# A transformer layer on one core: the first unit's keys, queries and maxima moved by 0/1 matrices instead of by DRAM, x and weights given turned, projections moved into the cycles

## What is computed

```python
x = _layernorm(x + attention(x))      # 32 query heads of width 16, 8 groups of keys and values, causal
x = _layernorm(x + ffn(x))

# attention: q = x Wq, k and v = x Wkv; scores = q k^T, upper triangle left out
# weights = softmax(scores / 4); out = (weights v) Wo + bo
# ffn:
h = einsum('bsd,nrd->nbsr', x, lora_A)
lora_out = einsum('nbsr,nor->bso', h, lora_B * 2 * lora_weights)
out = einsum('bsd,od->bso', x, W) + bias + lora_out
```

## Time and profile before

| | us |
|---|---|
| median of 3 runs (344.4 to 345.73) | 344.89 |
| the profiled execution | 345.44 |
| its span, first to last instruction | 343.7 |
| PE busy, share of the span | 327.0, 95% |
| DVE busy | 256.6, 75% |
| ACT busy | 219.9, 64% |
| POOL busy | 122.7, 36% |

### The profile page before, as it was taken

How to read it: one execution, slowest core, us unless ns; L and a number is a source line. 1 busy time by engine, 2 the same in 40 slices (tenths; PEclk the granted TensorE clock), 3 DMA queues, 4 the chain that set the end, 5 groups by cost and what they waited for, 6 DMA issues and landing times.

```text
span 343.7 us, 7378 instructions
## 1 busy us (share of the span) xinstructions
PE 327.0 (95%) x2584; PEld 180.8 (53%) x2585; DVE 256.6 (75%) x786; ACT 219.9 (64%) x414; POOL 122.7 (36%) x251
## 2 busy tenths in 40 slices
PE   7897989999999999999999999999999999999993
PEld 3674645555555454454454454544545545458882
DVE  2427788798889988978989889799888971037664
ACT  3672265676667768766847858588587686962331
POOL 2364233476455445511321114121141122321553
PEclk9999999999999999999999999999999999999999
DMA  7939948432450111010010010000000000000002
GB/s 217 267 121 194 340 115 97 109 97 83 136 141 14 36 50 47 2 49 0 3 47 32 3 48 3 1 32 3 1 2 1 16 18 3 2 10 23 0 31 93
DMA packets 21316, 21.38 MB, mean 62 GB/s; under 512 B 6112, under 2 KB 17312, under 8 KB 21280
## 3 DMA queue, kind: packets, MB, share of 16 engines
q1 hardware_dynamic: 21280, 20.92, 23.1%
HBM read 14.68 MB, written 6.03 MB: 60 GB/s over the span
## 4 chain that ended last, share of the span: by engine, by line
PE 81%; SPq 4%; DVE 4%; DMA 4%; ACT 3%; issue 3%; POOL 1%; POOLq 0%; DVEq 0%; ACTq 0%
PE PS L1195 20%; PE PS L1053 18%; PE PS L1031 18%; PE PS L1217 17%; SPq L468 2%; PE PS L1123 2%; PE PS L1115 2%; DMA TC<-in_L_attn_Wkv_dram 2%; ACT PB L772 1%; PE PS L1099 1%; DMA QS<-NMR 1%; PE PS L1101 1%; DMA QS<-scr_q 1%; PE PS L1040 1%; DVE scrap L829 1%
## 5 line engine op out<-in xcount | busy, mean ns | idle before, releaser
L772 ACT ACTIVATE PB<-PS 128x512 f32<-128x512 f32 x288 | 154.9, 600 | 55.9 <-PE PS L1217 54.5
L829 DVE CUSTOM_DVE_ANT_0 scrap<-PS,mask 128x128 bf16<-128x128 f32 (+3 forms) x256 | 111.6, 487 | 16.7 <-PE PS L1031 16.0
L1031 PE MATMUL PS<-KS,QS 96*128 96x512 bf16 (+3 forms) x384 | 107.2, 329 | 2.4 <-DMA QS<-scr_q 1.5
L1217 PE MATMUL PS<-QS,KS 99*128 99x512 bf16 x288 | 106.1, 381 | 0.8 <-ACT VX L673 0.3
L822 DVE TENSOR_REDUCE MX<-PS 128x1 f32<-128x512 f32 x128 | 82.1, 684 | 12.5 <-PE PS L1031 11.6
L648 POOL TENSOR_SCALAR_AFFINE_SELECT PB<-PB 128x256 f32<-128x256 f32 (+1 forms) x96 | 46.2, 483 | 105.5 <-ACT PB L772 102.5
L1195 PE MATMUL PS<-PB,VX 128*32 128x256 f32 (+1 forms) x1280 | 78.8, 364 | 0.6 <-ACT PB L772 0.3
L1031 PEld LDWEIGHTS PS<-KS,QS 96*128 96x128 bf16 x384 | 32.9, 98 | 47.9 <-issue 11.8
L1195 PEld LDWEIGHTS PS<-PB,VX 128*32 128x32 f32 x1280 | 33.5, 109 | 39.0 <-issue 16.1
L1053 PE MATMUL PS<-XT,WQ 128*128 128x512 f32 x144 | 41.5, 420 | 2.1 <-DVE WQ L966 1.5
L1217 PEld LDWEIGHTS PS<-QS,KS 99*128 99x128 bf16 x288 | 27.4, 98 | 30.3 <-ACT PB L772 7.1
(11 more groups left out here) (84 smaller groups left out, 270.2 us busy)
## 6 DMA issues: line engine op xcount, KB each, us to landing
scr_q<-parts SPq DMA_DIRECT2D x8, 384.0 KB, 2.9
QS<-scr_q SPq DMA_DIRECT2D x16, 192.0 KB, 3.5
X<-in_L_attn_x_dram SPq DMA_DIRECT2D x8, 256.0 KB, 5.7
QS<-scr_q SPq DMA_DIRECT2D x16, 128.0 KB, 3.3
out_dram<-TC SPq DMA_DIRECT2D x8, 256.0 KB, 2.0
QS<-scr_q SPq DMA_DIRECT2D x16, 64.0 KB, 3.1
...
```

The costliest lines, as they stand in the source:

```text
L772: nc.scalar.activation(PB[:, cyc % NP_BUF, k, :], PS[:, score_bank(e), :], ACT.Exp, scale=SCALE)\
L829: last = nc.vector.tensor_tensor_reduce(out=scrap[:, n % 2, (j - j0) * width:(j - j0 + 1) * width], in0=bank[:, j - j0, :], in1=mask[:, HT ...
L1031: last = nc.tensor.matmul(PS[:, CHUNK_BANK[n], k * width:(k + 1) * width], QS[0:ROWS, u % SLOTS, j, qb * P:(qb + 1) * P], KS[0:ROWS, g, k0 ...
L1217: nc.tensor.matmul(PS[:, score_bank(e), :], KS[0:NROW, u % G, kb * P:(kb + 1) * P], QS[0:NROW, u % SLOTS, heads[0]:heads[-1] + 1, s * HQ + ...
```

## The change

Five things change. (1) The host gives x turned as well as plain, Wq with its columns in the order of `parts`, Wkv as keys and values apart, lora_B and W turned, and the lora weights one to a partition. The `xT` and `bT` jobs and the transposes in `WE` go; ACT and DVE (first half) or POOL (second half) make the high and low part from x turned in SBUF, and plain x is loaded over it later, in cycles 8 to 16. (2) For unit 0, K and Q reach their rows by PE: POOL builds 0/1 selectors out of the identity, three matmuls of 96x512 place group 0's keys (`direct_keys`), twelve place the four heads (`direct_queries`), and 16 of 3x128 place the maxima (`direct_rows`), each copied by ACT or DVE from PSUM to `KS` or `QS`. The other units go through DRAM as before. (3) The last Q of the first half and V's transposes of the second move from the opening into cycles 2 and 6, the other fillers of `LATER` follow in cycles 5 to 17. (4) `WE` is one float32 matmul; DVE adds W, ACT copies the high part two cycles later and POOL subtracts the low part. (5) The idle matmuls behind `xT` and before cycle 0 go; the maxima of units 2 and 3 are turned one cycle later; Wo, LoRA and bias loads, and the splits of Wo and x, stand in other cycles.

The diff, cut to what the text speaks of:

```diff
-        return (FIRST[u] - (LEAD if u > 1 else 2)) if u else -1
+        return (FIRST[u] - (LEAD if u > 3 else 2)) if u else -1
...
-    PLAN_A = [(("xT", 0, c), 0) for c in range(NC)]
-    PLAN_A += [(("K", 0, 0), 0), (("Q", 0, 0), 0), (("V", 0, 0), 0), (("Q", 0, 1), 0), (("VT", 0, 0), 0)]
-    PLAN_A += [(("xT", 1, c), 0) for c in range(NC)]
-    PLAN_A += [(("Q", 0, 2), 5), (("K", 1, 0), 11), (("V", 1, 0), 13), (("Q", 0, 3), 15), (("VT", 1, 0), 16)]
+    PLAN_A = [(("K", 0, 0), 0), (("Q", 0, 0), 0), (("V", 0, 0), 0), (("Q", 0, 1), 3), (("VT", 0, 0), 4),
+              (("Q", 0, 2), 9), (("K", 1, 0), 11), (("V", 1, 0), 14)]
...
-    ROWS0_AFTER = 15
-    LATER = [("Q", 1, c) for c in range(NC)] + [("bT", 0, 0)] + [("WE", 0, c) for c in range(NC)]
+    LATER = [("Q", 0, 3), ("Q", 1, 0), ("VT", 1, 0), ("Q", 1, 1), ("WE", 0, 0), ("Q", 1, 2), ("WE", 0, 1),
+             ("Q", 1, 3), ("WE", 0, 2), ("WE", 0, 3)]
...
-    FILL = dict(zip((2, 5, 8, 11, 13, 14, 17, 20, 22), LATER))
+    FILL = dict(zip((2, 5, 6, 8, 10, 11, 13, 14, 16, 17), LATER))
...
-    LORA_AT, W_AT, SCALE_AT = (1, 2, 4, 5), (7, 10), 7
...
+    WO_AT, LORA_AT, W_AT, SCALE_AT, X_AT = (1, 2), 3, (5, 7), 8, (8, 10, 13, 16)
...
+        SELS = SEL.bitcast(BF16).rearrange("p (j a r) -> p j a r", j=REP + 1, a=NPART)
+        SEL_Q, SEL_K = SELS[:, 0:REP, :, :], SELS[:, REP, :, :]
+        XR = X[:, :, :].rearrange("p b d -> p (b d)").rearrange("p (c t) -> p c t", c=NC)
...
+            sp.dma_start(wk_raw, wkv[0].rearrange("(c p) n -> p c n", p=P)).then_inc(wk_in, 16)
+            load_turned(0)
             wq_v = wq.rearrange("(c p) n -> p c n", p=P)
             sp.dma_start(wq_raw[:, :, 0:P], wq_v[:, :, 0:P]).then_inc(wq_in, 16)
+            sp.dma_start(wv_raw, wkv[1].rearrange("(c p) n -> p c n", p=P)).then_inc(wv_in, 16)
...
+            load_turned(1)
             for n in range(PROJ_A):
-                if JOB[PROJ[n]] == ROWS0_AFTER + 1:
-                    move_maxima(0)
                 parts_to_dram(n)
                 if n == 1:
-                    load_keys(0, slice(0, 2), ks_first)
-                    load_queries(0)
                     load_queries(1)
-                    load_keys(0, slice(2, G), ks_in[0])
+                    load_keys(0, slice(1, G), ks_in[0])
                 if n == 2:
-                    sp.dma_start(wo_raw, wo.rearrange("(c p) n -> p c n", p=P)).then_inc(wo_in, 16)
-                if n == 3:
                     load_queries(2)
                     load_queries(3)
-                if n == 4:
+                if n == 3:
                     load_queries(4)
             load_keys(1, slice(0, G), ks_in[1])
             for cyc, (u, s, p) in enumerate(CYCLES):
-                if cyc in LORA_AT:
-                    c = LORA_AT.index(cyc)
-                    sp.dma_start(b_raw[:, c, :, :], lora_b[:, c * P:(c + 1) * P, :]
-                                 .rearrange("n p r -> p n r")).then_inc(ab_in, 16)
-                if cyc == LORA_AT[0]:
-                    sp.dma_start(coef[:, :], lora_w.partition_broadcast(P)).then_inc(ab_in, 16)
+                if cyc in WO_AT:
+                    c = slice(2 * WO_AT.index(cyc), 2 * WO_AT.index(cyc) + 2)
+                    sp.dma_start(wo_raw[:, c, :], wo.rearrange("(c p) n -> p c n", p=P)[:, c, :]).then_inc(wo_in, 16)
+                if cyc == LORA_AT:
+                    sp.dma_start(coef[:, :], lora_w).then_inc(ab_in, 16)
                     sp.dma_start(a_raw, lora_a.rearrange("n r d -> (n r) d")).then_inc(ab_in, 16)
+                    sp.dma_start(bT, lora_b).then_inc(ab_in, 16)
+                    sp.dma_start(bo_bc, bo.partition_broadcast(P)).then_inc(bo_in, 16)
+                    sp.dma_start(bias_bc[:, :], bias.partition_broadcast(P)).then_inc(bo_in, 16)
+                if cyc in X_AT:
+                    for c in range(2 * NC):
+                        sp.wait_ge(*x_split(c // NC, c % NC))
+                    for b in range(2 * X_AT.index(cyc), 2 * X_AT.index(cyc) + 2):
+                        sp.dma_start(X[:, b, :], x_v[b // TB][:, b % TB, :]).then_inc(x_back, 16)
...
+            link(nc.gpsimd.memset(SEL, 0.0))
+            for a, runs in enumerate(((0, 1, 2), (3, 4), (5,))):
+                for k in runs:
+                    nc.gpsimd.tensor_copy(SEL_K[:, a, k * HD:(k + 1) * HD], keys_of).then_inc(sel_ready, 1)
+            for a, runs in enumerate(((0, 3, 5), (1, 4), (2,))):
+                for k in runs:
+                    nc.gpsimd.tensor_copy(SEL_Q[:, :, a, k * HD:(k + 1) * HD], heads_of).then_inc(sel_ready, 1)
+            pool.wait_ge(sel_ready, 12)
+            constant(nc.gpsimd.memset(KS[ROWS:NROW, :, :].rearrange("p g t -> p (g t)").bitcast(F32), ONE_ONE), 5)
+            constant(nc.gpsimd.memset(VX[:, :, :, HD:2 * HD], 1.0), 6)
+            pool.wait_ge(wv_high, 1)
+            nc.gpsimd.tensor_tensor(WQ[:, 1, :, D + KD:D + 2 * KD], wv_raw,
+                                    WQ[:, 0, :, D + KD:D + 2 * KD].bitcast(F32), ALU.subtract).then_inc(wv_split, 1)
...
+            def split_w(c):
+                pool.wait_ge(we_high, c + 1)
+                nc.gpsimd.tensor_tensor(WEL[:, c, :], w_raw[:, c, :], WE[:, c, :].bitcast(F32), ALU.subtract)\
+                    .then_inc(we_split, 1)
...
+            act.wait_ge(wk_in, 16)
+            nc.scalar.activation(WQ[:, 0, :, D:D + KD], wk_raw, ACT.Copy).then_inc(wk_high, 1)
+            for c in range(NC):
+                x_high_half(0, c)
+            wq_high_half(0)
+            act.wait_ge(wv_in, 16)
+            nc.scalar.activation(WQ[:, 0, :, D + KD:D + 2 * KD], wv_raw, ACT.Copy).then_inc(wv_high, 1)
+            act_job(JOB["K", 0, 0])
+            middle_part(0)
+            wq_high_half(1)
+            act_job(JOB["Q", 0, 0])
+            middle_part(1)
+            direct_keys()
+            wq_high_half(2)
+            wq_high_half(3)
+            for j in (0, 2):
+                direct_queries(j)
+            act_job(JOB["V", 0, 0])
+            for c in range(NC):
+                x_high_half(1, c)
+                if c == 1:
+                    act_job(JOB["Q", 0, 1])
+                    middle_part(2)
+            act_job(JOB["VT", 0, 0])
+            act_job(JOB["Q", 0, 2])
+            middle_part(3)
+            act_job(JOB["K", 1, 0])
+            middle_part(4)
+            direct_rows(0, first_row)
+            direct_rows(2, nm_rows)
+            act_job(JOB["V", 1, 0])
...
+                    nc.vector.tensor_tensor(w_raw[:, c, :], bank, w_raw[:, c, :], ALU.add).then_inc(job_freed, 1)
...
+            dve.wait_ge(wk_high, 1)
+            nc.vector.tensor_tensor(WQ[:, 1, :, D:D + KD], wk_raw, WQ[:, 0, :, D:D + KD].bitcast(F32), ALU.subtract)\
+                .then_inc(wk_split, 1)
+            for c in range(NC):
+                x_low_half(0, c)
+            dve.wait_ge(wq_high, 1)
+            nc.vector.tensor_tensor(wq_part(1, 0), wq_part_raw(0), wq_part(0, 0).bitcast(F32), ALU.subtract)\
+                .then_inc(wq_split, 1)
...
+                if JOBS[n] == ("V", 0, 0):
+                    for j in (1, 3):
+                        dve.wait_ge(moved, 2 + j)
+                        nc.vector.tensor_copy(QS[0:ROWS, 0, j, :], PS[0:ROWS, DIRECT_BANKS[j], :]).then_inc(moved_dve, 1)
+                if JOBS[n] == ("K", 1, 0):
+                    for j in (1, 3):
+                        dve.wait_ge(nm_turned, j + 1)
+                        nc.vector.tensor_copy(QS[ROWS:NROW, 0, j, :], PS[ROWS:NROW, DIRECT_BANKS[j], :])                            .then_inc(odd_rows, 1)
...
+            def direct(lhs, slot, bank):
+                for a in range(NPART):
+                    last = nc.tensor.matmul(PS[0:ROWS, bank, :], lhs[:, a, :], parts[:, slot, a, :],
+                                            start=(a == 0), stop=(a == NPART - 1))
+                last.then_inc(moved, 1)
+            def direct_keys():
+                pe.wait_ge(parts_ready, 1)
+                pe.wait_ge(sel_ready, 12)
+                direct(SEL_K, 0, MISC)
+            def direct_queries():
+                pe.wait_ge(parts_ready, 2)
+                for j in range(REP):
+                    if DIRECT_BANKS[j] == MISC:
+                        pe.wait_ge(moved_act, 1)
+                    direct(SEL_Q[:, j, :, :], 1, DIRECT_BANKS[j])
+            def direct_rows():
+                pe.wait_ge(nm_parts, 1)
+                pe.wait_ge(max_read, UNIT_CHUNKS[1])
+                for j in range(REP):
...
+                        last = nc.tensor.matmul(PS[ROWS:NROW, DIRECT_BANKS[j], qb * P:(qb + 1) * P],
+                                                NMP[:, 0, qb, :, j], ident_bf[:, :], start=True, stop=True)
+                    last.then_inc(nm_turned, 1)
...
+                    if JOBS[n] == ("V", 1, 0):
+                        if part == 0:
+                            direct_rows()
+                            continue
+                        if part == 1:
```

(22 more changed lines are left out.)

260 lines of the change are left out of this document (131 added, 129 removed).

## The result

The changed kernel takes **353.06 us** (median of 6 runs, 350.4 to 355.65), the kernel before 344.61 in the same set (343.65 to 345.73): a ratio of 1.0254 (95% interval 1.0218 to 1.0289). It is slower by 8.5 us, where 8.4 us less were forecast. The profiled execution took 355.65 with a span of 353.9, 10.2 more than before.

A forecast was written before the change was run, and what follows sets the result against it. Behind the opening, PE's queue of work was taken as the bound, DVE as runner-up. Gains of 6.5+2.7-0.8 = 8.4 us took the profiled 345.44 to 337.0, and the median to 336.5; range 332 to 341.

The forecast's parts named there:

- Part one: Opening: without x's transposes and unit 0's DRAM trip, the first score chunk comes at 20.3 us, 8.8 earlier.
- rival (4): Opening: PE's own order sets the first chunk, so only removed work counts: gain 5.5, 339.4 us; chance 0.03.
- the rule quoted in the prediction: DVE subtracts and POOL operations reading SBUF exclude each other: V up to 2 us late, time some 1.2 us longer, 337.7.
- Part two: First chunk to cycle 0: maxima at 32.3, PE stands 31.2 to 33.7, cycle 0 at 37.4, 8.2 us earlier.
- Part three (a): Cycle 0 to unit 1's turn: fewer maxima done, turn 6.7 us after cycle 0, gain falls to 7.1.
- (b): Unit 1's turn to cycle 3: SP is free sooner, 6.1 us instead of 7.1, gain 8.0.
- Part three (c): Before cycle 6: SP's queue with five loads delays unit 2's maxima, PE waits 1 to 2 us, gain 7.0.
- Part three (d): Cycle 6: V's four transposes move there and cost 0.5 us, leaving a gain of 6.5.
- Part four: Cycles 7 to 24: removed transposes less one added Q give PE 2.7 us; 0.8 charged for DVE's queue.
- Rival (3): Opening: granted clock falls and stays low up to cycle 0, kernel ends 11 us slower, at 356; chance 0.04.
- Rival (2): Cycles 7 to 24: DVE becomes the bound, the 2.7 vanish, its extra subtract costs 0.7: 339.9 us; chance 0.2.

The follow-up runs named there:

- e9: Changed kernel with the five LoRA and bias loads in cycle 5, plus POOL waiting out DVE's small copy of the first maxima: 348.18 us.
- e4: Changed kernel with the five loads in cycle 5, the ten jobs set apart, and idle matmuls in PE's first two waits: 343.94 us.
- e1: Changed kernel with the five loads of LoRA and biases issued in cycle 5 instead of cycle 3: 348.66 us.
- e5: Changed kernel with only the two broadcast loads (bo and bias) moved from cycle 3 to cycle 5: 348.54 us.
- e2: Changed kernel with the ten jobs between score chunks at other cycles, no projection right behind a product: 351.85 us.
- e6: e4 plus four idle 512-column matmuls ahead of each of the four products: 346.44 us.
- e8: e4 with first half's last Q replacing 11 idle matmuls, nine jobs in the previous kernel's cycles, maxima of units 2 and 3 three cycles ahead: 339.02 us.
- e11: e1 with a planner rule changed: a job behind another job takes a bank of its own: 345.47 us.
- e12: e8 with the planner rule of e11, a bank of its own for a job behind a job: 338.57 us.

## Why the prediction was wrong, step by step

The forecast for the profiled execution was 337.0 and it took 355.65. The 18.6 us between lie so, by the first matmuls of the cycles: 2.8 up to cycle 0, 2.1 from 0 to 3, 4.3 from 3 to 6, 1.8 from 6 to 7, 7.5 from 7 to 24, none behind.

- **Part one was right.** First chunk 20.3 forecast, 20.76 measured. The short cut by PE works, rival (4) is out. V waited for POOL only 0.3 us, so the collision of the rule quoted in the prediction cost little there; it struck at the maxima's copy instead.
- **Part two was right up to the maxima** (32.3, measured 32.88), and PE stood as named there, 2.8 us. Cycle 0 came at 40.20, not 37.4: 0.6 from the maxima, 0.6 from the copy that ran beside POOL's subtract (e9), and the rest, 1.6, from the 1.2 GHz stretch (from the turned rows to cycle 0 5.4 us; in e4, at full clock, 3.9; forecast 3.7). This 1.6 is a term that the sum had at nothing. I had named the wait "the longest idle that the new order makes", and put no price on what follows it.
- **Part three (a)** was right in size: the turn 6.7 after cycle 0, measured 6.8. **(b)** the turn to cycle 3 was put at 6.2; it took 8.25 with the second fall of the clock, 6.6 in e1 and e4 without. The terms written there, 0.4+0.6+3x0.62+3.63, make 6.5 and not 6.1; with the right sum the step agrees with the runs at full clock, and of the regained 0.9 some 0.5 are left.
- **Part three (c) is the step whose mechanism was right and whose size was wrong.** Place, queue and the five loads are as described, to a tenth of a microsecond up to the first of the three issues. The term "landing 1.9 to 3.6", taken as 2.5, measured 5.99, and the three issues 2.05 for 1.25. The wait was 4.5 us where 1 to 2 were forecast. e5 shows that the two broadcasts of 256 KB are the cause, in issue and landing. The upper end of the range, 3.6, was itself the landing of rows behind six key loads of 128 KB and LoRA's A in the old trace, and the sum took a value below it. That trace had a hint of more, the landing of those key loads themselves (KB each, us to landing, 45 to 70 us), but no row with a load spread over the partitions in front of small ones:

```profile
KS<-scr_k SPq DMA_DIRECT2D x6, 128.0 KB, 4.7
```

- **Part three (d) was right**: the four transposes were put at 0.5. In e1, with the changed kernel's table and the clock full there, cycle 6 takes 0.2 more than before (2.77 for 2.53 us). The changed kernel's 4.84 is these 2.77 and 2.1 of the low clock, for which the sum had nothing. Only in e2's table, which e4 and e6 share, V's turn waits 1.0 for a bank (in e4 cycle 6 takes 1.4 more); at cycle 13 (e8) the 1.3 us that it loses there is back by cycle 15.
- **Part four failed in its working, not only in a size.** From cycle 7 to 24, 1.9 less was forecast, and the changed kernel takes 5.6 more (65.92 for 60.31). I summed PE's work and DVE's work, and the planner's table was taken as neutral. It is not: jobs in neighbouring cycles make PE wait for DVE (e2: 5.8 us in cycles 9 to 17, 3.5 of them net; e11: the bank alone 1.7). The last sentence of the prediction names this, "if the planner's new distribution of chunks leaves PE waiting for banks anywhere behind cycle 6", as what would make it wrong; it had no price and no chance. The sum itself is off as well: its terms make 2.2 to 2.6, not 2.7. The transposes of W and B were put at 4.0, and V's turn, which stands in these cycles in e8, at 0.5: PE's busy time fell by 2.5 (e8), and the time by 1.8. e4 against e8 gives what the additional projection of these cycles costs in e4's table, 3.5 us (62.08 for 58.54), forecast 2.8; the other jobs stand in other cycles too, so it is not the projection alone. So even with the jobs set apart (e4) the balance of part four is +1.8 and not -1.9.
- **Rival (3), slower by the clock, chance 0.04**, gave nearly the right time (356), by luck: in the changed kernel's trace no clock fell before 35 us, and the falls, behind the waits at 32, 45 and 67 us, cost about 2 us by the medians, not 19. Its mechanism is not out, though. In e2's trace the clock fell in the opening, behind a wait of 1.80 us for x, for 3.4 us and not up to cycle 0; the 18 projection matmuls behind it took 6.18 us for 4.53. The eight idle matmuls that the change took out stood there, and no run puts them back. Rival (2) gives 0.7 more in cycles 7 to 24 without any gain, near to the +1.8; by e6 DVE is a partial bound there. The side was wrong because a wait of 4.5 us, jobs bunched by a table, and the clock behind waits stood against a gain in the opening that is real. Where the gain was kept (e12) the kernel is at 338.6, inside the forecast's range; what is missing to 336.5 is about the later cycle 0 (in e8 2.6 us behind the forecast). These kernels have a projection in the opening and idle matmuls that the changed kernel has not, so they do not confirm the sum.

It stays open why the clock falls behind a wait in one execution and not in another, what part of the loss of bunched jobs beyond the bank is DVE's queue and what the missing chunk banks, and whether bytes or the spreading of a row made the two loads heavy.
